# Attention and gated feed-forward, float32 on one core: early stores by halves of the heads, V products over two steps, later feed-forward weights, and VectorE's two sums moved by one burst

## What is computed

```python
Q = split(x); K = split(x @ Wk + bk); V = split(x @ Wv + bv)      # V: 1024 wide
attn = softmax(Q @ K.T + causal_mask)
o = merge(attn @ V)
x = layernorm(x + x + gelu(o) @ Wf + bf)                          # exact gelu
gate = x @ wg.T; up = x @ wu.T                                    # int weights / 127, 768 wide
x = layernorm(x + (silu(gate) * up) @ wd.T)
```

## Time and profile before

| | us |
|---|---|
| median of three runs (1868.45 to 1873.46) | 1868.6 |
| profiled execution | 1864.17 |
| its span | 1862.4 |
| busy: TensorE, VectorE, GpSimd, ScalarE | 1768.4, 1397.4, 1220.3, 1050.2 |
| mean granted clock of TensorE | 0.982 |

### The profile page before, as it was taken

The page is one execution under the profiler, slowest core; times in us unless marked ns, Lnnn a source line. Parts: engine busy times, 40 slices in busy tenths (PEclk is TensorE's granted clock), DMA queues, the critical chain, the costliest instruction groups (busy, mean ns, idle before and its releaser), DMA issues. The chain is left out here.

```text
span 1862.4 us, 37593 instructions
## 1 busy us (share of the span) xinstructions
PE 1768.4 (95%) x10304; PEld 966.1 (52%) x10304; DVE 1397.4 (75%) x3411; ACT 1050.2 (56%) x1374; POOL 1220.3 (66%) x1151
## 2 busy tenths in 40 slices
PE   7799999999999999999999999888889999999996
PEld 5444444444444444444444444333367767676763
DVE  3777877778777777878778777887467878787864
ACT  2355656656656666656656566555554656565552
POOL 3378888888888888888888898889711222222221
PEclk9899999999999999999999999999999999999998
DMA  8865655565564655655565564564376565766500
GB/s 279 254 191 149 191 150 174 154 188 156 161 199 138 183 169 146 195 147 172 170 175 156 166 190 129 155 149 135 81 173 188 162 181 168 176 171 170 170 23 23
DMA packets 260959, 303.15 MB, mean 163 GB/s; under 512 B 28048, under 2 KB 177680, under 8 KB 260880
## 3 DMA queue, kind: packets, MB, share of 16 engines
q1 hardware_dynamic: 260880, 302.19, 57.2%
HBM read 174.20 MB, written 127.93 MB: 162 GB/s over the span
## 5 line engine op out<-in xcount | busy, mean ns | idle before, releaser
L774 POOL TENSOR_TENSOR weight_sum<-weight_sum,weights 128x512 f32<-128x512 f32 (+3 forms) x448 | 728.4, 1626 | 161.0 <-DVE weight_sum L1308 120.8
L1122 ACT ACTIVATE weights<-ring 128x1024 f32<-128x1024 f32 x576 | 570.7, 1026 | 210.8 <-PE ring L818 208.3
L818 PE MATMUL o_acc<-weights,v_pair 128*64 128x512 f32 (+3 forms) x3072 | 583.2, 500 | 17.5 <-POOL weights L732 15.2
L809 POOL TENSOR_TENSOR h_lo<-hidden,h_hi 128x512 f16<-128x512 f32 x96 | 114.2, 1191 | 391.1 <-ACT h_hi L1065 391.1
L1273 DVE TENSOR_REDUCE part_max<-ring 128x2 f32<-128x1024 f32 x256 | 301.0, 1217 | 89.9 <-PE ring L818 89.9
L818 PEld LDWEIGHTS o_acc<-weights,v_pair 128*64 128x64 f32 x3072 | 188.2, 136 | 301.8 <-issue 263.6
L1282 DVE CUSTOM_DVE_ANT_0 scrap<-ring,causal 128x128 bf16<-128x128 f32 (+3 forms) x512 | 225.3, 486 | 114.6 <-PE ring L818 114.3
L1282 DVE CUSTOM_DVE_ANT_0 scrap<-ring,causal,part_max 128x256 bf16<-128x256 f32 (+3 forms) x512 | 251.3, 547 | 70.8 <-PE ring L818 70.5
L818 PE MATMUL ring<-q_stack,k_stack 50*128 50x512 f32 (+3 forms) x1536 | 266.8, 386 | 29.8 <-DVE part_max L1273 16.9
L818 PE MATMUL ring<-k_stack,q_stack 48*128 48x512 f32 (+3 forms) x1536 | 259.2, 375 | 7.3 <-DMA k_stack<-k_rows 3.2
L818 PE MATMUL ring<-wf_sb,g 128*128 128x256 f32 x1024 | 230.5, 380 | 1.8 <-ACT g L1143 0.9
(11 more groups left out here) (123 smaller groups left out, 2069.5 us busy)
## 6 DMA issues: line engine op xcount, KB each, us to landing
v_pairs<-v_unit SPq DMA_DIRECT2D x64, 512.0 KB, 3.5
v_pair<-v_pairs SPq DMA_DIRECT2D x64, 512.0 KB, 5.1
o_heads<-o_pair SPq DMA_DIRECT2D x64, 512.0 KB, 3.2
g<-o_heads SPq DMA_DIRECT2D x16, 2048.0 KB, 8.1
den_wide<-reciprocals SPq DMA_DIRECT2D x32, 1024.0 KB, 13.1
q_stack<-q_rows SPq DMA_DIRECT2D x128, 192.0 KB, 3.7
k_stack<-k_rows SPq DMA_DIRECT2D x128, 192.0 KB, 4.3
q_rows<-x_hi SPq DMA_DIRECT2D x30, 512.0 KB, 3.6
```

The costliest lines, as they stand in the source:

```text
L774: pool.tensor_tensor(dst, other, weights(t), ALU.add).then_inc(s_add, 1)
L809: pool.tensor_tensor(h_lo[:, f], h32[f % 2][:], h_hi[:, f], ALU.subtract).then_inc(s_hl, 1)
L818: return nc.tensor.matmul(o, l, r, start=start, stop=stop)
L1122: nc.scalar.activation(W[i][:], bank_of("t", i)[:], ACT.Exp).then_inc(s_w, 1)
```

## The change

Five edits.

1. The early stores are issued by half: chunk c = 0 is features 0 to 127, which are heads 0 to 7. The first halves of Q and K of both units count on a semaphore of their own, `s_row0`, and the first stacks wait for that alone. K's second halves are stored after the first stacks are asked for. ScalarE's waits that guarded the whole rows get a wait on `s_row0` beside them.
2. The early V products go to bursts 0 to 3 of step 0 and 1 to 4 of step 1; TensorE enters loop B after six instead of eight copies; SyncE stores the first two V tiles of unit 1 right after it has asked for the stacks of pair 1, ahead of the rows of Q of the next unit.
3. Wf is loaded in step 4, the integer weights at r = 58 ahead of the first g. `wi_in` moves to the place of the second g and x, so their load moves from r = 62 to r = 65 and waits for the casts, which move from step 1 to step 64.
4. VectorE's BEGIN moves from the end of burst 2 to the end of burst 3, CARRY in burst 4 from ahead of the maxima of s6 to behind them. (In the order of its queue: s3 BEGIN s4 s5 CARRY s6 becomes s3 s4 s5 BEGIN s6 CARRY.)
5. GpSimd's mask 2 comes before `add(1)`.

```diff
@@ -68,9 +68,9 @@
 JOB_AT = (4, 5, 6)
-EARLY_V = ((0, 1), (2, 3), (4,), (5,), (6,), (7,))
-EARLY_BANK = (0, 1, 0, 1, 0, 1, 1, 1)
-EARLY_WAIT = (0, 0, 1, 2, 3, 4, 6, 7)
+EARLY_AT = (0, 1, 2, 3, 7, 8, 9, 10)
+EARLY_BANK = (0, 1, 0, 1, 1, 0, 1, 0)
+EARLY_WAIT = (-1, 0, 1, 2, 4, 4, 5, 6)
 YSCALE = 2048.0
@@ -152,8 +152,13 @@
         pctx.close()
-        g = [sb(f"g{i}", [P, HC, U], F32) for i in range(2)]
-        xn = [sb(f"xn{i}", [P, UT, D], F32) for i in range(2)]
+        g = [sb("g0", [P, HC, U], F32)]
+        xn = [sb("xn0", [P, UT, D], F32)]
+        ictx = ExitStack()
+        wi_in = [sb(f"wi_in{i}", [P, DC * FH], I32, ictx) for i in range(3)]
+        ictx.close()
+        g.append(sb("g1", [P, HC, U], F32))
+        xn.append(sb("xn1", [P, UT, D], F32))
         dn0 = sb("den_wide0", [P, HC, U], F32)
@@ -184,9 +189,6 @@
         lctx.close()
-        ictx = ExitStack()
-        wi_in = [sb(f"wi_in{i}", [P, DC * FH], I32, ictx) for i in range(3)]
-        ictx.close()
         abctx = ExitStack()
@@ -271,6 +273,7 @@
         s_kst = sem("k_stored")
+        s_row0 = sem("early_rows_of_first_heads_stored")
         s_vst = [sem(f"v_tile_stored{i}") for i in range(UT)]
@@ -409,16 +412,23 @@
-            def store_early(a):
+            def store_half(rows, parts, stored, a, c):
+                for m, split in enumerate(parts):
+                    sp.dma_start(rows.rearrange("m b h d t -> m b (h d) t")[m, a // 2, P * c:P * (c + 1),
+                                                                           a % 2 * U:a % 2 * U + U],
+                                 split[:, c].bitcast(F32)).then_inc(stored, 16)
+            def store_early(a, c):
                 sp.wait_ge(s_xes, a + 1)
-                store_rows(qd, (hi, hi, lo), s_qst, a)
-            def store_early_k(a):
+                store_half(qd, (hi, hi, lo), s_qst if c else s_row0, a, c)
+            def store_early_k(a, c):
                 hi, lo = ((k_hi, k_lo), (ke_hi, ke_lo))[a]
-                sp.wait_ge(s_eks, DC * (a + 1))
-                store_rows(kd, (hi, lo, hi), s_kst, a)
+                sp.wait_ge(s_eks, DC * a + c + 1)
+                store_half(kd, (hi, lo, hi), s_kst if c else s_row0, a, c)
@@ -466,7 +476,10 @@
                 slot = r % RING
-                if r % 4 == 0:
+                if r == 0:
+                    sp.wait_ge(s_row0, 16 * 6 * ALONE)
+                elif r % 4 == 0:
@@ -559,6 +572,9 @@
                     load_shifts(r - 1, n - 1)
+                if r == 0:
+                    for i in range(2):
+                        store_early_v(1, i)
                 if r == 1:
@@ -582,10 +598,8 @@
                     store_q(a)
-                if r == 0:
-                    load_rest()
-                    for i in range(2):
-                        store_early_v(1, i)
+                if r == 4:
+                    sp.dma_start(wf_sb[:], Wf.rearrange("(c p) n -> p c n", p=P)).then_inc(s_w_in, 16)
                 if r == PAIRS - 6:
@@ -598,10 +612,13 @@
                     sp.wait_ge(s_rst, 16 * 2)
+                    load_rest()
                     load_g(0, 0)
                     load_dn(0, 0)
-                if r == PAIRS - 2:
+                if r == PAIRS + 1:
+                    sp.wait_ge(s_wrest, 3)
                     load_g(1, 0)
@@ -631,10 +648,6 @@
-                sp.wait_ge(s_wks, 1)
-                sp.wait_ge(s_wvs, 1)
-                sp.wait_ge(s_xes, 2)
-                sp.dma_start(wf_sb[:], Wf.rearrange("(c p) n -> p c n", p=P)).then_inc(s_w_in, 16)
                 sp.dma_start(wi_in[0][:].rearrange("p (c n) -> p c n", c=DC),
@@ -649,12 +662,16 @@
             sp.dma_start(bf_sb[:], bf.partition_broadcast(P)).then_inc(s_w_in, 16)
-            store_early(0)
-            store_early(1)
-            store_early_k(0)
-            store_early_k(1)
+            store_early(0, 0)
+            store_early(0, 1)
+            store_early(1, 0)
+            store_early_k(0, 0)
+            store_early_k(1, 0)
+            store_early(1, 1)
             sp.wait_ge(s_krows, 2 * RING)
             load_stacks(0, 0)
+            for a in range(ALONE):
+                store_early_k(a, 1)
             load_x(ALONE, True)
@@ -784,8 +801,8 @@
                 if now:
+                    mask(2, *m)
                     add(1, *m)
-                    mask(2, *m)
                     add(2, *m)
@@ -847,7 +864,7 @@
             pe.wait_ge(s_eks, DC * ALONE)
-            pe.wait_ge(s_eev, NV)
+            pe.wait_ge(s_eev, NV - 2)
             pe.wait_ge(s_const, 4)
@@ -863,9 +880,12 @@
                     else:
-                        pe.wait_ge(s_eev, NV + 5)
+                        pe.wait_ge(s_eev, NV + 3)
                 else:
                     wait_job_copied(pe, a, i - 1)
+                    if NBURST * r + b == EARLY_AT[-1] + 1:
+                        pe.wait_ge(s_eev, 2 * NV)
                 if b in JOB_AT[:2] and r >= LEAD:
@@ -991,12 +1011,14 @@
                         denominators(back, n + back - r)
-                    if r == 0:
-                        for v in EARLY_V[b]:
-                            if EARLY_WAIT[v]:
-                                pe.wait_ge(s_eev, NV + EARLY_WAIT[v])
-                            job(DC + v, oo[EARLY_BANK[v]][:], xe_hi, xe_lo, s_ej)
+                    if NBURST * r + b in EARLY_AT:
+                        v = EARLY_AT.index(NBURST * r + b)
+                        pe.wait_ge(s_eev, NV + EARLY_WAIT[v])
+                        if v == 5:
+                            wait_job_copied(pe, ALONE, 2)
+                        job(DC + v, oo[EARLY_BANK[v]][:], xe_hi, xe_lo, s_ej)
                     job_beside(r, it, b)
@@ -1082,6 +1104,9 @@
                     act.wait_ge(s_job, NJ * (a - ALONE))
+                if first:
+                    act.wait_ge(s_row0, 16 * 6 * ALONE)
                 act.wait_ge(s_qst, 16 * 3 * a)
@@ -1146,12 +1171,12 @@
                 for b in range(NBURST):
-                    if r == 0 and b >= 1 or r == 1 and b == 0:
-                        for v in EARLY_V[b - 1]:
-                            copy_early_v(1, v, oo[EARLY_BANK[v]][:])
+                    if NBURST * r + b - 1 in EARLY_AT:
+                        v = EARLY_AT.index(NBURST * r + b - 1)
+                        copy_early_v(1, v, oo[EARLY_BANK[v]][:])
                     if r == LEAD and b == 0:
-                        act.wait_ge(s_wrest, 3)
+                        act.wait_ge(s_row0, 16 * 6 * ALONE)
                         act.wait_ge(s_qst, 16 * 3 * ALONE)
@@ -1330,18 +1355,18 @@
                         k_part2(ended[1], ended[0], oo[0][:])
-                    if b == 4 and LEAD <= r < PAIRS + LEAD:
-                        carry_sum(r - LEAD, n - LEAD)
                     for what, j in uses(b):
                             top(j, r, n)
-                    if b == 2 and LEAD <= r < PAIRS + LEAD:
+                    if b == 4 and LEAD <= r < PAIRS + LEAD:
+                        carry_sum(r - LEAD, n - LEAD)
+                    if b == 3 and LEAD <= r < PAIRS + LEAD:
                         begin_sum(r - LEAD, n - LEAD)
                         norm(0, 0, range(2 * b - 4, 2 * b))
-                    if b == 5 and r == 1:
+                    if b == 0 and r == PAIRS:
                         ffn_weights()
```

## The result

| | before | after |
|---|---|---|
| median, us | 1867.5 (1862.8 to 1873.5) | 1882.4 (1870.8 to 1890.9) |
| ratio to before, 95% interval | | 1.0071 [1.0057, 1.0085] |
| span of the profiled execution | 1862.4 | 1880.8 |

A forecast was written before the change was run, and what follows sets the result against it. It took VectorE and the shifts to bound the second step, TensorE the middle, and a ring through GpSimd and VectorE the last eight pairs. −10 −12 +0 +1 +0 = −21, less 1 of doubt: −20, 1868.6 to 1848.6; range 1835 to 1865.

The forecast's parts named there:

- Head, −10: Start of the kernel, up to the fourth step: 10 us saved, with 6 and 12 as ends.
- (a): Head, first heads' rows stored first: the first stacks' wait ends earlier, a gain of 1.1 us, no more.
- (b): Head, K's second-half stores ahead of the V stores: V stores move later, TensorE stands 2 to 3 us in the first step.
- (c): Head, four V products instead of eight in the first step: 5.7 us leave it; net, second step 3 to 4 us earlier.
- (d): Head, second step: SyncE reaches the shifts at about 57, they land near 63; third step starts at about 65, not 73.67.
- Middle, −12: Steps with projections: the wait for maxima goes, −0.9 us per four steps, −12 in all; ends −17 and +6.
- the K projection behind it may lose 0.3 us: Middle, fourth step, with the split of x on GpSimd: CARRY stays stretched and the K projection may lose 0.3 us.
- Eight pairs, 0: Last eight pairs, without projections: mask 2's wait ends but the pace stays, so no gain; ends −4 and +5.
- The ring: Last eight pairs: cycle of mask 1, V product, scores, maxima, BEGIN, CARRY and GpSimd, summed to 18.4 us against 18.4 measured.
- Late weights, +1 (0 to +4): Weights loaded at steps 4 and 58: one step's shifts 1 to 2 us late, +1; VectorE's casts at step 64 cost 0.
- Loop C, 0: Feed-forward stage: second g lands 3 to 7 us later, mostly absorbed before the third g; 0 (−3 to +5).
- GpSimd becomes the bound: Rival: BEGIN and CARRY wait out additions, CARRY 3.7 us late, two-projection steps lose 1.4 each; about +17, 1885.6; chance 0.08.

The follow-up runs named there:

- b4: Edits 1, 2 and 5 without edit 3, VectorE's sums in the old order: feed-forward weights loaded in step 0 and cast in step 1; 1864.5 us, ratio 0.9981.
- c4: Edit 3 (late weights) alone on the kernel before; 1861.7 us, ratio 0.9974.
- c3: The changed kernel, all five edits, with GpSimd's x_low made on 16 of 512 tokens only; 1849.1 us, ratio 0.9903.
- a4: The changed kernel with GpSimd's x_low moved ahead of its additions 2 and 3; 1870.8 us, ratio 1.0017.
- a1: The changed kernel without edit 4: VectorE's sums BEGIN and CARRY at their old places, the other four edits kept; 1858.0 us, ratio 0.9939.
- a3: The changed kernel with CARRY right behind BEGIN, ahead of the maxima of s6; 1862.5 us, ratio 0.9978.
- b1: Edits 1, 2 and 3 alone, with VectorE's sums and GpSimd's mask 2 where the kernel before has them; 1860.2 us, ratio 0.9956.
- a2: The kernel before with edit 4 alone: BEGIN behind s5, CARRY behind s6; 1898.3 us, ratio 1.0163.
- b2: The changed kernel with BEGIN back at its old place ahead of maxima 4, CARRY still behind s6; 1911.3 us, ratio 1.0226.

## Why the prediction was wrong, step by step

- **Head, −10: right in size (−8.1), half wrong in cause.** Terms (a), (b) and (c) happened, and so did the early shifts of (d); but b4 and c4 show that (a) to (c) are worth nothing in the end that stands out of the head's scatter and that the shifts' landing, not their issue, was the bound. V products came at 74.68, between before's 82.01 and the 72 forecast.
- **Middle, −12: measured +17.8. The failed step is the sentence "the K projection behind it may lose 0.3 us".** I followed CARRY's 1.9 us of delay (measured 2.1) to masks 0 and 1, where I found 2.0 us of slack, and never followed it to x_low in the fourth step. There the slack was 0.35 us. What the runs show in place of the 0.3 is 2.0 us: the K projection starts 3.84 us after the V products before it (690.36 to 694.20) instead of 1.87, and the step takes 21.90 against 19.92 in c3. The step lost only 1.0 against before, since without x_low's lateness edit 4 shortens it by about 1.0 (20.88 against 19.92 in c3, with the reserve made there). With the two rows of before, the delay would have given 1.9 − 0.35 = 1.5 us in each of 13 rounds, +20 instead of +4: the middle would have come to +4, of the right sign, and the whole forecast to about −4 us, still faster. The late x_low isn't mended by its place in the queue (a4), only by the time it takes (c3): what I left out is 2.3 us of work of an engine that was already late. The 0.2 us in each of two steps for masks are 0.5 in the fourth step, but a1, with the old order of the sums, has 0.4 of that too: it is edit 5's price, for which I had charged nothing. Only the gain of 0.7 in the third step is as forecast. Three slow steps, 9 us, were in no term.
- **Eight pairs, 0: measured +8.5.** The ring that I added up to 18.4 is 19.07 in steady steps, and 18.20 with the old order of the sums and mask 2 first. The failed step here is the ring's VectorE half: in step 58 it takes 8.1 us from the end of mask 1 to the second-half additions, where I had 7.2 (BEGIN takes 1.56 us there, I had 1.1). a3, with CARRY ahead of the maxima of s6, has those additions 0.69 us earlier in its step 58 and the step at 18.37. Two steps take 19.8, beside the late weights (TensorE waits 2.64 us for the shifts once), and step 63 takes 21.05, 2.0 of it for the casts. And mask 2 first is worth something there: 3.1 us without late weights (before against b4, which also has edits 1 and 2), 5.7 with them (b1 against a1). With CARRY late the sums look alike (156.2 in a2, 156.0 after), but a2 has no late weights: its eight steps take 19.5 each against 19.07 in the steady ones of after, so mask 2 first is worth 0.45 us a step, and the late weights and casts use up the 3.5 us.
- **Late weights, +1 (0 to +4): right at the upper end.** a1 against b4: 3.7 us in the last eight pairs. About half of it is the queue (step 59), the other half VectorE's casts (step 63), which I had put at 0 because VectorE stands idle there: it is GpSimd that the casts hold up. With the old place of mask 2 the late weights cost more, 5.8 us (c4 against before). The wait of 1 to 2 us for the shifts of one step was 2.64.
- **Loop C, 0: measured +0.3.** The exchange of den_wide's wait for the third g's is as described.
- **Rivals.** "GpSimd becomes the bound" had the right sign (1885.6 against 1882.4) and a part of the mechanism, but placed it in the two-projection steps beyond 2.0 us of slack. The loss lies in the x_low steps, below that point. It got 0.08 because I judged it by GpSimd's idle time before CARRY; that idle time is the wait for CARRY itself, and moving CARRY moves it along. (In the chances, 0.50 + 0.14 + 0.07 and two thirds of 0.21 are 0.85, not 0.84; nothing hangs on it.)

The sum, on the profiled spans: −8.1 + 17.8 + 8.5 + 0.3 = +18.5, and 1880.8 − 1862.4 = 18.4.

## What to carry to other kernels

When a step is moved later on one engine, list every operation that the engine behind it runs until the chain has slack again, the rare ones too (one step in four), and take for each the distance from its end to its first reader; the smallest distance is the slack, not that of the row that happens to be nearest. To move that one operation up helps only if the ones behind it have slack: in a4 the wait went from x_lo to the masks. An edit that removes a wait by making another engine late should be tried in its halves: here the late half cost 53 us and the other repaired 29 of it, and neither is visible in the whole. An engine's idle time ahead of the moved operation is no reserve if it is the wait for that operation.

## What the runs showed of the hardware

**A VectorE sum waits out GpSimd's operation.** In the step shown above x_low ends at 691.72 + 2.34 = 694.06 and CARRY, begun at 692.32, at 695.15: 1.09 us after it. Before, the same sum gives 764.90 + 2.36 = 767.26 and 768.35: 1.09 again, and CARRY with nothing beside it takes 1.22. So it does its work after x_low has ended. All 13 CARRYs beside x_low of either trace end 1.08 to 1.09 us after it, and of the 60 sums of after that begin within another GpSimd operation every one ends about 1.1 us after that operation; the 54 with nothing beside them take 1.21 to 1.22. The Trainium skill, SBUF — State Buffer, section "SBUF: two separate sides", has whichever of the two starts first keep the shared ports for its whole instruction, and these rows agree. The forecast had this rule turn the middle's −12 into −5. On average over the middle BEGIN takes 1.50 us after and 1.31 before, CARRY 1.62 and 1.68, together 0.13 us more in each of 52 steps, 7 us of VectorE's time; that is no account of +17.8. And it isn't BEGIN's new place as such: in a3, where it has that place and GpSimd is less late, it takes 1.22.

**The granted clock fell in three steps of the changed kernel.** Windows of step 16, then of step 28, both x_low steps of after (columns as in the earlier trace rows), and one group of V products in step 16:
```profile
357.34:382.31 24.97, 22.34 (x116) 10.76 (x116) 17.75 (x41) 12.84 (x16) 21.41 (x23) 0.86 0.57 159
...
604.16:626.06 21.90, 19.28 (x116) 9.33 (x116) 17.76 (x41) 12.84 (x16) 19.86 (x20) 1.00 0.64 182
```
```profile
363.33 1.94 PE L835 MATMUL o_acc<-weights,v_pair 128*64 128x512 f32 x8
367.16 0.49 PE L835 MATMUL o_acc<-x_hi,wk_hi 128*128 128x512 f32 x1 [1.90 <-POOL x_lo L770]
...
370.95 2.83 PE L835 MATMUL o_acc<-weights,v_pair 128*64 128x512 f32 x8
```
The same 116 matmul records take 22.34 us at a mean granted clock of 0.86 and 19.28 at 1.00: 3.1 us per step, with part of step 16 at 1.2 instead of 2.4 GHz. Ahead of it TensorE had stood 1.90 us for x_lo; but the same wait stands in step 28, where the clock stayed. No such step stands in the middle of before, a4 or c3, which wait less there; b4, without any wait for x_lo, had such a step too (step 44, 23.5 us), and b2 five (8, 20, 28, 36 and 44, 23.4 to 23.5 us against 21.8); there TensorE had stood 1.0 to 1.1 and then 0.4 us for maxima just before the clock fell. a2, with waits of up to 1.1 us, had none. What decides it is open. Three to four such steps more or less are as much as the scatter of the changed kernel (1870.8 to 1890.9), which is an argument and not shown.
